# Clearing each layer's semaphores on GpSimd inside the following layer, with one barrier between two layers

## The chip, the cores and the metric

The kernel runs on one core of one Trainium2 chip. The metric is the time of one execution on the device, in microseconds. Before the change three runs took 1180.79, 1188.72 and 1182.0 us; their median is 1182.0 us.

A core has five engines, each with its own instruction queue: TensorE (PE in the profile; its weight loads have a row of their own, PEld), VectorE (DVE), ScalarE (ACT), GpSimd (POOL) and SyncE (SP, which here only starts DMAs). [...]

## What is computed

The reference is a stack of eight residual blocks on an input of 16 sequences x 128 tokens x 128 features: four times an attention over a context (16 heads), each followed by a feed-forward block of another kind. Each block reads the normalised rows of what the blocks before left:

```
x = x + _L0_xattn_ref(_layernorm(x), ctx_1024, mask, ...)   # masked attention
x = x + _L0_ffn_ref(_layernorm(x), ...)                      # top 2 of 8 experts, 2 iterations
x = x + _L1_xattn_ref(_layernorm(x), ctx_1024, ctx_1024, ...)  # a temperature per head
x = x + _L1_ffn_ref(_layernorm(x), ...)                      # top 1 of 14 experts
x = x + _L2_xattn_ref(_layernorm(x), ctx_1024, ...)          # self, then cross attention
x = x + _L2_ffn_ref(_layernorm(x), ...)                      # product keys
x = x + _L3_xattn_ref(_layernorm(x), ctx_1024, ctx_1024, ...)  # causal attention
x = x + _L3_ffn_ref(_layernorm(x), ...)                      # gated low-rank layers
return x
```

## The kernel before

x stays in on-chip memory throughout. `build` calls one function for each block, in the order of the reference; the first attention calls `first_layernorm` ahead of itself, so there are nine stages: the first row norm, l0, l0f, l1, l1f, l2, l2f, l3, l3f (the names that the tiles carry as a prefix; all attentions use the tile prefix `l_`).

Each stage has this frame:

- `with cleared_semaphores(nc) as new_semaphore` (line 33). It hands out the stage's semaphores. When the stage is left, GpSimd clears them all (`nc.clear_and_free_semaphores(taken)`, line 42) and gives their numbers back, and then all five engines meet in a barrier (`nc.all_engine_barrier()`, line 43).
- Inside it `nc.Block()`. Each engine gets its own instruction list for the stage. When the block is left, all five engines meet in a barrier too. Its instructions carry the line of the stage's `with` statement in the trace: 215 for the first row norm, 266 for l0 and l3, 1225 for l0f, 603 for l1, 1726 for l1f, 2161 for l2, 2460 for l2f, 1990 for l3f.

A barrier goes like this: each engine executes a DRAIN, which waits until its earlier instructions are done, and raises one semaphore; POOL waits for four of these, then raises a second semaphore, and each other engine goes on when it sees that one. I call this last step the release.

So two barriers stand between two stages, with the clear between them. The second is there because the next stage takes the same semaphore numbers again, and none may count on one before it is zero.

What stands around the boundary is much the same for all stages. A stage ends in DVE's last row statistics (`RowStats.take`, lines 120 and 123). The next begins with `RowNorm`: DVE normalises rows (line 179) and PE turns them (line 188). Three rows are normalised on ACT (line 193), for which POOL first makes `away` (lines 165 and 168). POOL also makes the last four rows' scale (lines 128 and 131). Behind that POOL's own work for the stage starts: the setting of buffers to constants (`MEMSET`, lines 342 to 347 in l0 and l3, 680 to 685 in l1, 1308 to 1313 in l0f, 2717 and 2718 in l2f), an addition (line 2240) in l2, the scatter of rows (line 1798) in l1f, and nothing in l3f. In l0, which has its row norm in a stage of its own, these MEMSETs come first.

In l1f, POOL scatters rows to DRAM, copies expert weights (line 1805), waits till the results are in DRAM, and gathers them back with 16 indirect DMAs (line 1811).

Of the kernel before, what the change touches and what calls it, by code (L numbers as in the profile page):

```python
# [31 lines left out]
@contextmanager  # L32
def cleared_semaphores(nc):

    taken = []

    def new_semaphore(name):
        taken.append(nc.alloc_semaphore(name=name))
        return taken[-1]

    yield new_semaphore
    nc.clear_and_free_semaphores(taken)
    nc.all_engine_barrier()
# [94 lines left out]
class RowNorm:  # L138
# [24 lines left out]
    def pool(self, pool):  # L163
        m, known = self.m, slice(0, RowStats.KNOWN)
        self.nc.gpsimd.tensor_tensor(self.away[:, known], m["row_mean_var"][:, known, 0], m["row_rstd"][:, known],
                                     ALU.mult).then_inc(self.away_made, 1)
        pool.wait_ge(self.away_made, 1)
        self.nc.gpsimd.tensor_scalar(self.away[:, known], self.away[:, known], -1.0, None, ALU.mult) \
            .then_inc(self.away_made, 1)
        self.row_stats.scale(pool, RowStats.KNOWN, B, rms=self.rms_gain is not None).then_inc(self.rstd_made, 1)  # L170

# [40 lines left out]
def first_layernorm(nc, m, tag, meanwhile):  # L212

    x, xnT, identity = m["x"], m["xnT"], m["identity"]
    with cleared_semaphores(nc) as new_semaphore, ExitStack() as ctx:
# [43 lines left out]
def cross_attention(nc, m, w, tag, meanwhile, masked_keys=False, causal=False, first=None, keys=None):  # L259
# [6 lines left out]
    with cleared_semaphores(nc) as new_semaphore, ExitStack() as ctx:  # L266
# [71 lines left out]
        def _(pool):  # L338
            if norm is not None:
                norm.pool(pool)  # L340
            for r in range(2):
                nc.gpsimd.memset(neg_max[r][:, :], 0.0).then_inc(ready, 1)
# [255 lines left out]
def tempered_attention(nc, m, w, tag, meanwhile):  # L598
# [4 lines left out]
    with cleared_semaphores(nc) as new_semaphore, ExitStack() as ctx:  # L603
# [577 lines left out]
def refine_experts(nc, m, w, tag, meanwhile):  # L1181
# [43 lines left out]
    with cleared_semaphores(nc) as new_semaphore, ExitStack() as ctx:  # L1225
# [492 lines left out]
def top1_experts(nc, m, w, tag, meanwhile, keys_ahead, values_ahead, last_keys, ahead_of):  # L1718
# [7 lines left out]
    with cleared_semaphores(nc) as new_semaphore, ExitStack() as ctx:  # L1726
# [67 lines left out]
        def _(pool):  # L1794
# [6 lines left out]
            for j in range(NT):  # L1801
                e = pool.value_load(tile_u[0:1, j:j + 1], min_val=0, max_val=E - 1)
                if j >= RING:
                    pool.wait_ge(y_stored, j - RING + 1)
                nc.gpsimd.tensor_copy(held[j % RING][:, :], w["experts"][:, bass.ds(e, 1), :].rearrange("p a f -> p (a f)")) \
                    .then_inc(fetched, 1)
            pool.wait_ge(scattered_early, 16 * EARLY)
# [175 lines left out]
def gated_lora(nc, m, w, tag, meanwhile):  # L1983
# [6 lines left out]
    with cleared_semaphores(nc) as new_semaphore, ExitStack() as ctx:  # L1990
# [160 lines left out]
def two_attentions(nc, m, w, tag, meanwhile, fold_of, keys_ahead, values_ahead):  # L2151
# [9 lines left out]
    with cleared_semaphores(nc) as new_semaphore, ExitStack() as ctx:  # L2161
# [291 lines left out]
def product_keys(nc, m, w, tag, meanwhile):  # L2453
# [6 lines left out]
    with cleared_semaphores(nc) as new_semaphore, ExitStack() as ctx:  # L2460
# [9 lines left out]
        spare, taken = m["spare"], [m["fold"].shape[1]]  # L2470
# [549 lines left out]
def build(nc, dram, where, out):  # L3020

    with ExitStack() as ctx:
# [37 lines left out]
        m["out"] = out  # L3060
# [43 lines left out]
        for name, layer, tag, options, meanwhile in run:  # L3104
# [12 lines left out]
            layer(nc, m, by_group[tag], tag, meanwhile, **options)  # L3117

# [16 lines left out]
```

## Time and profile before

| | us |
|---|---|
| three runs | 1180.79, 1188.72, 1182.0 |
| their median | 1182.0 |
| the profiled execution | 1187.32 |
| its span, first to last instruction | 1185.6 |
| busy in it: PE | 948.0 |
| DVE | 740.0 |
| ACT | 583.8 |
| POOL | 414.4 |

The span is what the trace covers; 1.7 us of the profiled execution lie around it. Busy time is the sum of an engine's instructions; barrier, semaphore and DRAIN instructions are not in it. They are found by asking for the line that issued them.

### The profile page before, as it was taken

What the parts mean: (1) busy time and instruction counts of PE and PEld (TensorE: products, weight loads), DVE (VectorE), ACT (ScalarE), POOL (GpSimd) and SP (SyncE); (2) the same over time, 40 slices, a digit from 0 to 9 for tenths busy, and PEclk for the clock granted to TensorE, in tenths of its full rate; (3) what the DMA queues carried; (4) which work ended last, traced back from release to release, by engine and by line L of the source; (5) the groups of instructions that cost most, each with busy time, mean ns of one, the idle gap of its engine ahead of it and who ended that gap; (6) DMA issues with size and microseconds to landing.
All of it is one profiled execution on the core that took longest, in us unless ns stands there. A gap on an engine that the chain in (4) does not pass through costs nothing. (4 is left out here: it accounts for less than half of the span.)

```text
span 1185.6 us, 26637 instructions
## 1 busy us (share of the span) xinstructions
PE 948.0 (80%) x10747; PEld 617.9 (52%) x10777; DVE 740.0 (62%) x2026; ACT 583.8 (49%) x956; POOL 414.4 (35%) x426
## 2 busy tenths in 40 slices
PE   3999799998999986998798781777556677479997
PEld 1577433443333433677676381445345555446776
DVE  3587747557455564654375233478899999636764
ACT  3365365535555344554563460377555555325442
POOL 4230300000000011676201656246578878623340
PEclk9799699998999998999898796899778987789997
DMA  6000000000000007000000132100000000000001
GB/s 268 1 3 2 19 1 0 1 1 0 1 1 1 0 1 288 10 2 3 2 3 2 36 110 56 72 1 1 1 2 2 2 2 3 2 1 2 2 2 37
DMA packets 15434, 27.95 MB, mean 24 GB/s; under 512 B 1104, under 2 KB 13264, under 8 KB 14544
## 3 DMA queue, kind: packets, MB, share of 16 engines
q1 hardware_dynamic: 14288, 24.14, 5.7%
q0 software_dynamic: 1024, 2.10, 0.6%
q8 instruction: 87, 1.43, 0.5%
q14 instruction: 35, 0.29, 0.1%
HBM read 20.33 MB, written 5.90 MB: 22 GB/s over the span
## 5 line engine op out<-in xcount | busy, mean ns | idle before, releaser
L1324 PE MATMUL l0f_ctl<-l1f_in,l0f_in 128*128 128x512 f32 x320 | 145.7, 599 | 0.5
L128 POOL TENSOR_SCALAR row_var_eps<-row_mean_var 128x12 f32<-128x12 f32 (+2 forms) x16 | 3.7, 230 | 358.5 <-DVE row_mean_var L123 357.7
L548 DVE TENSOR_REDUCE l_neg_max<-l_ring 128x4 f32<-128x512 f32 x128 | 82.1, 684 | 66.1 <-PE l_ring L410 65.6
L507 ACT ACTIVATE l_probs<-l_scores 128x1024 f32<-128x1024 f32 x64 | 65.6, 1025 | 82.2 <-PE l_scores L418 82.2
L2663 ACT COPY l2f_blocks_sb<-l2f_right_t_sb 32x1024 f32<-32x1024 f32 x64 | 66.8, 1044 | 68.2 <-DVE l2f_right_t_sb L2804 33.8
L1324 PEld LDWEIGHTS l0f_ctl<-l1f_in,l0f_in 128*128 128x128 f32 x320 | 61.7, 193 | 71.5 <-issue 70.2
L2593 PE MATMUL l2f_given_ps<-l2f_blocks_sb,l2f_left_t_sb 128*32 128x128 f32 x1024 | 47.8, 364 | 33.1 <-ACT l1f_in L2669 22.6
L698 POOL TENSOR_TENSOR l_squares<-l_exps 128x1024 f32<-128x1024 f32 x32 | 60.6, 1895 | 29.8 <-ACT l_exps L953 29.8
L2593 PEld LDWEIGHTS l2f_given_ps<-l2f_blocks_sb,l2f_left_t_sb 128*32 128x32 f32 x1024 | 42.8, 150 | 47.1 <-issue 46.9
L1045 DVE TENSOR_REDUCE l_neg_max<-l_scores 128x8 f32<-128x1024 f32 x32 | 39.2, 1225 | 43.4 <-PE l_scores L750 43.4
L368 POOL TENSOR_SCALAR_AFFINE_SELECT l_probs<-l_probs 128x1024 f32<-128x1024 f32 x32 | 35.0, 1094 | 64.1 <-ACT l_probs L507 64.1
L1597 DVE TENSOR_SCALAR l0f_halt<-l0f_halt 128x512 f32<-128x512 f32 x8 | 3.4, 427 | 78.8 <-ACT l0f_halt L1483 78.8
L1590 DVE SCALAR_TENSOR_TENSOR l1f_in<-l0f_index,l0f_in,l0f_hidden 128x512 f32<-128x512 bf16 x64 | 43.5, 747 | 12.3 <-ACT l0f_index L1464 11.1
L2743 POOL TENSOR_TENSOR l2f_factors_sb<-l2f_factors_sb,l1f_in 128x512 f32<-128x512 f32 x32 | 48.0, 1500 | 0.0
L953 ACT ACTIVATE l_exps<-l_scores 128x1024 f32<-128x1024 f32 x32 | 32.8, 1025 | 30.0 <-PE l_scores L756 29.8
L410 PE MATMUL l_ring<-l_k_heads,l_q_all 32*128 32x256 f32 x256 | 41.0, 441 | 7.9 <-issue 3.2
L1324 PE MATMUL l0f_work<-xnT,l0f_in 128*128 128x512 f32 (+2 forms) x88 | 45.0, 684 | 1.3 <-ACT xnT L204 0.7
L750 PE MATMUL l_scores<-l_k_heads,l_q_all 32*128 32x256 f32 x256 | 36.8, 402 | 10.0 <-DVE l_neg_max L1045 8.3
L2569 PE MATMUL l2f_sim_ps<-l1f_in,xnT 128*128 128x512 f32 x32 | 21.6, 764 | 28.8 <-DVE l1f_in L2772 28.8
L1446 ACT ACTIVATE l0f_hidden<-l0f_work,l0f_in 128x512 f32<-128x512 f32 (+1 forms) x40 | 27.3, 686 | 29.0 <-PE l0f_work L1324 29.0
L992 ACT ACTIVATE l_exps<-l_scores 128x1024 f32<-128x1024 f32 x32 | 31.0, 1021 | 20.7 <-PE l_scores L837 20.7
L756 PE MATMUL l_scores<-l_q_all,l_k_heads 32*128 32x128 f32 x512 | 37.7, 286 | 1.8 <-ACT l_exps L953 1.8
(458 smaller groups left out, 2610.2 us busy)
## 6 DMA issues: line engine op xcount, KB each, us to landing
l1f_in<-in_l1f SPq DMA_DIRECT2D x1, 4580.0 KB, 13.4
l0f_in<-in_l0f SPq DMA_DIRECT2D x1, 2302.5 KB, 8.9
l0f_in<-in_l2f SPq DMA_DIRECT2D x1, 2080.5 KB, 18.7
l1f_in<-in_l2u SPq DMA_DIRECT2D x1, 2048.0 KB, 8.6
sorted_rows<-first_in SPq DMA_DIRECT2D x1, 1856.0 KB, 11.2
l1f_sorted<-sorted_rows SPq DMA_DIRECT2D x7, 256.0 KB, 4.6
expert_rows<-l1f_sorted SPq DMA_DIRECT2D x7, 256.0 KB, 2.2
x_in<-in_x SPq DMA_DIRECT2D x1, 1024.0 KB, 5.0
```

The source lines that it names most:

```text
L410: ins1 = mm(score_bank(b, half, g)[:, :, t, :], q_all[r, b, t, :], k_heads[r, b, t, :, :], start=not causal, stop=True, skip_group_check=True)
L507: nc.scalar.activation(probs[c % 2][:, 2 * pair:2 * pair + 2], scores2[:, :, :, :, :], ACT.Exp, scale=SCORE_SCALE).then_inc(exp_done, 1)
L548: ring.free(V.tensor_reduce(out, score_bank(b, half, g), AX.X, ALU.max, negate=True), ("score", b, half, g))
L698: nc.gpsimd.tensor_tensor(squares[c % 2][:, pair], e, e, ALU.mult).then_inc(squared, 1)
L750: ins1 = mm(scores1[:, g, :, t, :], q_all[r, b, t, :], k_heads[r, b, t, :, :], start=True, stop=True, skip_group_check=True)
L756: ins2 = mm(scores2[:, g, j, t, :], k_heads[r, c, t, j, :], q_all[r, c, t, :], start=True, stop=True, skip_group_check=True)
L1045: V.tensor_reduce(out, scores1[:, :, :, :, :].rearrange("p g j t s -> p (g j) t s"), AX.X, ALU.max, negate=True).then_inc(max_taken, 1)
L1324: return nc.tensor.matmul(out, lhs, rhs, start=start, stop=stop)
L1590: ins = STT(chosen[c % 2][:, k, p, :], index[k][:, c % 2, :], w["row_expert"][:, p:p + 1], hidden[c % 2][:, p, :], ALU.is_equal, ALU.mult)
L2593: ins = mm(given_ps[K * j:K * j + K, s, :, :], left_t[b % 2][:, 8 * j + s, :], blocks[:, 8 * j + s, :, :], start=True, stop=True)
L2663: A.copy(blocks[rows, :, u, :], right_t[rows, :, :]).then_inc(blocks_made, 1)
L2743: TT(value, value, kept[:, side, :, :], ALU.mult).then_inc(cut_made, 1)
```

## The change

A stage's semaphores are no longer cleared when the stage is left, and the barrier of line 43 goes. The list is kept in `m["semaphores_to_clear"]`, and the next stage clears it on POOL: in the stages with a row norm of the usual kind at the end of `RowNorm.pool`, behind the four small instructions, and in l0 ahead of the MEMSETs. The next stage has other semaphore numbers, since the old ones aren't free before that. The last stage's are cleared after it, with one barrier behind, as before. l1f gets one more `drain` on POOL, between the copies of the expert weights and the wait for the DRAM writes.

```
-def cleared_semaphores(nc):
+def cleared_semaphores(nc, m):
     ...
     yield new_semaphore
-    nc.clear_and_free_semaphores(taken)
-    nc.all_engine_barrier()
+    assert not m["semaphores_to_clear"]
+    m["semaphores_to_clear"] = taken
+
+
+def clear_last_layers_semaphores(nc, m):
+    nc.clear_and_free_semaphores(m["semaphores_to_clear"])
+    m["semaphores_to_clear"] = []
 ...
         self.row_stats.scale(pool, RowStats.KNOWN, B, rms=self.rms_gain is not None).then_inc(self.rstd_made, 1)
+        clear_last_layers_semaphores(self.nc, m)
 ...
             if norm is not None:
                 norm.pool(pool)
+            else:
+                clear_last_layers_semaphores(nc, m)
             for r in range(2):
                 nc.gpsimd.memset(neg_max[r][:, :], 0.0).then_inc(ready, 1)
 ...
                 nc.gpsimd.tensor_copy(held[j % RING][:, :], w["experts"][:, bass.ds(e, 1), :].rearrange("p a f -> p (a f)")) \
                     .then_inc(fetched, 1)
+            nc.gpsimd.drain()
             pool.wait_ge(scattered_early, 16 * EARLY)
 ...
-        m["out"] = out
+        m["out"], m["semaphores_to_clear"] = out, []
 ...
             layer(nc, m, by_group[tag], tag, meanwhile, **options)
+        clear_last_layers_semaphores(nc, m)
+        nc.all_engine_barrier()
```

The eight `with cleared_semaphores(nc)` lines become `with cleared_semaphores(nc, m)`. The line numbers of the changed file are larger by 5 or more.

POOL's instructions from the end of l0 to the first work of l0f, before (a branch is the jump out of one block or into the next, ISA is the clear of a range of semaphores; DRAINs and barrier instructions are not listed):

```order
L266 UNCONDITIONAL_BRANCH
L42 ISA
L1305 UNCONDITIONAL_BRANCH
L165 TENSOR_TENSOR l0f_away<-row_mean_var,row_rstd 128x12
L168 TENSOR_SCALAR l0f_away<-l0f_away 128x12
L128 TENSOR_SCALAR row_var_eps<-row_mean_var 128x4
L131 TENSOR_TENSOR row_rstd<-row_var_eps,first_in 128x4
L1308 MEMSET l0f_choice 128x2048
```

and of the change:

```order
L272 UNCONDITIONAL_BRANCH
L1313 UNCONDITIONAL_BRANCH
L170 TENSOR_TENSOR l0f_away<-row_mean_var,row_rstd 128x12
L173 TENSOR_SCALAR l0f_away<-l0f_away 128x12
L133 TENSOR_SCALAR row_var_eps<-row_mean_var 128x4
L136 TENSOR_TENSOR row_rstd<-row_var_eps,first_in 128x4
L47 ISA
L1316 MEMSET l0f_choice 128x2048
```

The clear moved past the four small instructions, ahead of the first MEMSET. No other instruction of these changed its place.

POOL's instructions from the gather of l1f into l2, before:

```order
L1811 DMA l1f_rows<-expert_rows,l1f_place_u 128x128 x16
L128 TENSOR_SCALAR row_var_eps<-row_mean_var 128x12
L131 TENSOR_TENSOR row_rstd<-row_var_eps,first_in 128x12
L1726 UNCONDITIONAL_BRANCH
L42 ISA
L2223 UNCONDITIONAL_BRANCH
L165 TENSOR_TENSOR l_away_sb<-row_mean_var,row_rstd 128x12
L168 TENSOR_SCALAR l_away_sb<-l_away_sb 128x12
L128 TENSOR_SCALAR row_var_eps<-row_mean_var 128x4
L131 TENSOR_TENSOR row_rstd<-row_var_eps,first_in 128x4
L2240 TENSOR_TENSOR l_last_b_sb<-l_in 128x128
```

and of the change:

```order
L1820 DMA l1f_rows<-expert_rows,l1f_place_u 128x128 x16
L133 TENSOR_SCALAR row_var_eps<-row_mean_var 128x12
L136 TENSOR_TENSOR row_rstd<-row_var_eps,first_in 128x12
L1734 UNCONDITIONAL_BRANCH
L2232 UNCONDITIONAL_BRANCH
L170 TENSOR_TENSOR l_away_sb<-row_mean_var,row_rstd 128x12
L173 TENSOR_SCALAR l_away_sb<-l_away_sb 128x12
L133 TENSOR_SCALAR row_var_eps<-row_mean_var 128x4
L136 TENSOR_TENSOR row_rstd<-row_var_eps,first_in 128x4
L47 ISA x2
L2249 TENSOR_TENSOR l_last_b_sb<-l_in 128x128
```

The same move, and the clear is now of two ranges: the numbers of a stage no longer follow one another without a gap. Over the whole program there is one range in l0 and l0f, three in l2f, and two in each of the others and at the end. On PE, DVE, ACT and SP no listed instruction changes its place.

## Rows read from the trace of the kernel before

**Rows 1.** The page: span, then busy time and share of the span by engine.
```profile
span 1185.6 us, 26637 instructions
PE 948.0 (80%) x10747; PEld 617.9 (52%) x10777; DVE 740.0 (62%) x2026; ACT 583.8 (49%) x956; POOL 414.4 (35%) x426
```

**Rows 2.** Line 42, then 43, whole span: ns min/median/max, first to last start.
```profile
L42 POOLq EVENT_SEMAPHORE_RANGE_CLEAR  x9: 73/243/348, 17.1 to 1185.2; - x9
L43 POOLq EVENT_SEMAPHORE  x18: 17/17/17, 17.2 to 1185.5; - x18
L43 POOLq DRAIN  x9: 34/34/40, 17.2 to 1185.3; - x9
L43 DVEq EVENT_SEMAPHORE  x9: 21/21/21, 17.4 to 1185.5; - x9
```

**Rows 3.** Boundary l0 to l0f: block's release, line 42, second release.
```profile
L266 DVEq EVENT_SEMAPHORE  x1: 21/21/21, 130.1 to 130.1; - x1
L42 POOLq EVENT_SEMAPHORE_RANGE_CLEAR  x1: 178/178/178, 130.3 to 130.3; - x1
L43 DVEq EVENT_SEMAPHORE  x1: 21/21/21, 130.7 to 130.7; - x1
```

**Rows 4.** The same three at the boundary l2 to l2f.
```profile
L2161 DVEq EVENT_SEMAPHORE  x1: 21/21/21, 839.5 to 839.5; - x1
L42 POOLq EVENT_SEMAPHORE_RANGE_CLEAR  x1: 348/348/348, 839.7 to 839.7; - x1
L43 DVEq EVENT_SEMAPHORE  x1: 21/21/21, 840.3 to 840.3; - x1
```

**Rows 5.** The same three at the boundary first row norm to l0.
```profile
L215 DVEq EVENT_SEMAPHORE  x1: 21/21/21, 16.9 to 16.9; - x1
L42 POOLq EVENT_SEMAPHORE_RANGE_CLEAR  x1: 73/73/73, 17.1 to 17.1; - x1
L43 DVEq EVENT_SEMAPHORE  x1: 21/21/21, 17.4 to 17.4; - x1
```

**Rows 6.** Timeline, l0 to l0f: start, us, what [idle before <-releaser].
```profile
129.72 0.18 DVE L123 BATCH_NORM_AGGREGATE row_mean_var<-row_stats 128x2 f32<-128x6 f32 x1
130.81 3.95 DVE L179 TENSOR_SCALAR l1f_in<-x_in,row_mean_var,row_rstd 128x128 f32<-128x128 f32 x9 [0.91 <-PEq L43]
...
131.21 2.37 PE L188 MATMUL l0f_ctl<-first_in,l1f_in 128*128 128x128 f32 x9 [2.52 <-DVE l1f_in L179]
```

**Rows 7.** Timeline of POOL in l0f, then line 1570's wait on DVE.
```profile
136.03 0.13 POOL L1313 MEMSET l0f_half<- 128x1 f32 x1
144.80 1.65 POOL L1318 TENSOR_TENSOR l0f_gap_exp<-common_in,l0f_gap 128x8 f32<-128x8 f32 x1 [8.64 <-DVE l0f_gap L1566]
L1570 DVEq EVENT_SEMAPHORE  x2: 21/21/21, 145.0 to 186.9; - x2
```

**Rows 8.** Waits of POOL: line waited for: us in total, times, longest us.
```profile
POOL l_probs L368 <- ACT l_probs L507: 64.1, 32, 12.6
POOL l_rstd_sb L2230 <- DVE l_var_eps_sb L2426: 47.6, 10, 27.7
POOL l_max_all L690 <- DVE l_neg_max L1045: 18.3, 2, 13.4
POOL sorted_rows L1798 <- DVE l1f_place_u L1949: 16.3, 1, 16.3
POOL l1f_in L2723 <- DVE l1f_in L2758: 4.3, 1, 4.3
```

**Rows 9.** Timeline of l3's start: POOL's last MEMSETs, PE's first scores.
```profile
1050.86 0.17 POOL L347 MEMSET l_v<- 128x16 f32 x2
1055.55 0.38 PE L395 MATMUL l_ring<-common_in 128*128 128x512 bf16 x1 [1.04 <-ACT l_q_all L495]
```

**Rows 10.** Timeline of POOL in l1f, then DRAINs at the block's end (line 1726).
```profile
711.18 2.24 POOL L1805 COPY l1f_held<-l1f_in 128x642 f32 x3 [0.55 <-DVE l1f_sorted L1972]
718.90 1.01 POOL L1811 DMA_INDIRECT l1f_rows<-expert_rows,l1f_place_u  x1 [5.47 <-DMA expert_rows<-l1f_sorted]
L1726 POOLq DRAIN  x1: 5042/5042/5042, 739.0 to 739.0; - x1
L1726 DVEq DRAIN  x1: 406/406/406, 742.4 to 742.4; - x1
```

**Rows 11.** DRAINs of POOL at other blocks' ends.
```profile
L266 POOLq DRAIN  x2: 2379/2380/2382, 120.7 to 1154.6; - x2
```

**Rows 12.** Windows: us, then busy us of PE, PEld, DVE, ACT, POOL, PEclk, DMA, GB/s.
```profile
131.00:149.00 18.00, 15.10 (x63) 7.77 (x64) 16.38 (x67) 7.17 (x12) 6.38 (x9) 0.50 0.10 30
150.00:168.00 18.00, 15.57 (x44) 6.00 (x44) 9.87 (x15) 13.05 (x22) 0.00 (x0) 1.00 0.00 1
```

More of the change, by code:

```diff
@@ L214, in first_layernorm @@
     x, xnT, identity = m["x"], m["xnT"], m["identity"]
-    with cleared_semaphores(nc) as new_semaphore, ExitStack() as ctx:
+    with cleared_semaphores(nc, m) as new_semaphore, ExitStack() as ctx:
         def sem(name):
@@ L265, in cross_attention @@
     KINDS, AHEAD = len(kinds), 5 if keys is None else T
-    with cleared_semaphores(nc) as new_semaphore, ExitStack() as ctx:
+    with cleared_semaphores(nc, m) as new_semaphore, ExitStack() as ctx:
         def sb(name, shape):
@@ L602, in tempered_attention @@
     PARTS = ((0, 12), (12, B))
-    with cleared_semaphores(nc) as new_semaphore, ExitStack() as ctx:
+    with cleared_semaphores(nc, m) as new_semaphore, ExitStack() as ctx:
         def sb(name, shape):
@@ L1223, in steps @@
                 yield n, it, c, g, r, part
-    with cleared_semaphores(nc) as new_semaphore, ExitStack() as ctx:
+    with cleared_semaphores(nc, m) as new_semaphore, ExitStack() as ctx:
         def sb(name, shape, dt=F32):
@@ L1725, in top1_experts @@
     x, xnT, identity = m["x"], m["xnT"], m["identity"]
-    with cleared_semaphores(nc) as new_semaphore, ExitStack() as ctx:
+    with cleared_semaphores(nc, m) as new_semaphore, ExitStack() as ctx:
         def sb(name, shape, dt=F32):
@@ L1989, in gated_lora @@
     x, xnT, identity = m["x"], m["xnT"], m["identity"]
-    with cleared_semaphores(nc) as new_semaphore, ExitStack() as ctx:
+    with cleared_semaphores(nc, m) as new_semaphore, ExitStack() as ctx:
         def sb(name, shape):
@@ L2160, in two_attentions @@
              sorted((n + SKEW * c, c, name, a) for n, (name, a) in enumerate(STAGES) for c in range(NCH))]
-    with cleared_semaphores(nc) as new_semaphore, ExitStack() as ctx:
+    with cleared_semaphores(nc, m) as new_semaphore, ExitStack() as ctx:
         def sb(name, shape, dt=F32):
@@ L2459, in product_keys @@
     x, xnT, identity = m["x"], m["xnT"], m["identity"]
-    with cleared_semaphores(nc) as new_semaphore, ExitStack() as ctx:
+    with cleared_semaphores(nc, m) as new_semaphore, ExitStack() as ctx:
         def sb(name, shape):
```

## The prediction

> **What bounds the kernel now.** I read the page first, for what fills the span. No engine does: PE is busy 948.0 of 1185.6 us, DVE 740.0, POOL only 414.4 [rows 1]. The stages run strictly one after another, and each hands over through a point where all five engines stand still. So next I asked for the lines of that point, 42 (the clear) and 43 (the second barrier). Each occurs nine times [rows 2], once behind each stage. Then I looked at single boundaries.
>
> At the end of l0 DVE gets the release of the block's own barrier at 130.1 and the release of the second barrier at 130.7; between them lies a clear of 178 ns [rows 3]. DVE's last statistics start at 129.72 and its first work of l0f at 130.81, after 0.91 us of idling [rows 6]. Both are on the path: the statistics were the last work of l0, and the row norm that PE, ACT and all else of l0f wait for starts right behind the release. So at a boundary the time from the first release to the second adds to the span one to one, whichever engine was last before and whichever is first after.
>
> **What the change does, part by part.**
>
> *Removed: the time from release to release, at eight boundaries.* It has a fixed part and the clear. Three boundaries give 130.7 - 130.1 = 0.6 us with a clear of 0.178 [rows 3], 840.3 - 839.5 = 0.8 with 0.348 [rows 4], and 17.4 - 16.9 = 0.5 with 0.073 [rows 5]. Less the clear that leaves 0.42, 0.45 and 0.43 us, so 0.43 fixed. These three have the smallest and the largest clear of the nine, whose median is 0.243 [rows 2]. The removed time is 8 x (0.43 + 0.243) = 5.4 us. The starts are given to 0.1 us; if each difference were off by 0.1 in the same direction, the sum would be 4.6 or 6.2.
>
> The records of the removed instructions alone come to far less: one clear of 0.243, a DRAIN of 0.034, two semaphore instructions of 0.017 on POOL and the release of 0.021 [rows 2] make 0.33 us a boundary, 2.7 us for eight. The rest is time in which no record runs. The Trainium skill, Perfetto Trace Analysis, section Sequencer-only Instruction, says that a record holds only the execution, and that the wait and the spreading of a semaphore's new value to all engines are outside it. By that rule too the price is the one from release to release, and by records alone 2.7 us; the trace agrees with the rule, with 0.6 us between releases where the records make up about half.
>
> *Moved: the clears, onto POOL inside the next stage.* Each holds POOL for its own time, a DRAIN ahead of it, and a start: from the first release to the end of the clear it was about 0.2 + 0.348 us at the largest [rows 4], which I take as 0.55 us at most for one range, and somewhat more for two or three. POOL was itself released 0.5 to 0.8 us earlier, so in time its later work starts about where it did; in distance to its consumers, which all moved up, it is some 0.5 us late. What hides it, stage by stage:
> - l0f: the last MEMSET starts at 136.03, and the wait of DVE for it is executed at 145.0; POOL's next real work waits 8.64 us for DVE [rows 7].
> - l1, l1f, l2: behind the first small instructions POOL idles 13.4, 16.3 and 27.7 us for DVE, the longest waits of these three rows [rows 8].
> - l2f: 4.3 us of idle time for DVE [rows 8].
> - l3: the last MEMSETs start at 1050.86, and the first scores that need them at 1055.55, held up by ACT [rows 9]; that is 4.5 us. POOL's first causal mask then idles 12.6 us [rows 8].
> - l0's MEMSETs are like l3's, and l3f has no POOL work behind it.
>
> The smallest cover is 4.3 us against 0.5, so I cost the move at nothing. With the cover gone it would be up to 0.55 us each, 4.4 us for eight.
>
> *Added: the `drain` in l1f.* POOL's last copy ends at 711.18 + 2.24 = 713.4 (the three are back to back), and its next instruction starts at 718.90 because of a DMA [rows 10]. That is 5.5 us of cover. A DRAIN of POOL at a block's end takes 2.38 us behind a long instruction [rows 11] and 5.04 us in l1f behind the indirect DMAs [rows 10]. Bounds: nothing, if it only waits for the copies; 5.04 us, still under the cover. I take nothing. There is a possible gain in it. The DRAIN at l1f's end lasts from 739.0 to 744.0, while DVE's is over at 742.8 [rows 10], so this one boundary waits 1.2 us for POOL. If part of that long DRAIN is old business of the scatter that the new drain settles earlier, up to 1.2 us more is won. Nothing in the trace speaks for the scatter rather than the gather, which is the nearer in time, so I take 0 here too.
>
> *Added: a second range at the end of the program.* It is on the path. Between 0.07 and 0.35 us by the clears [rows 5, 4], but the total of semaphores is the same, so the low end: 0.1 us.
>
> **The sum.** 5.4 - 0.1 = 5.3 us. The profiled execution took 1187.32 us (span 1185.6 and 1.7 around it), so it would take 1182.0. That execution was 5.3 us above the median of the runs, 1182.0; taken from this median the sum gives 1176.7. The three runs and the profiled one have a mean of 1184.7, which gives 1179.4. Between these I take 1178.
>
> **The rivals.**
>
> *A. The clear isn't hidden.* A clear in the midst of a stage may hold up the semaphores that the other engines are using just then, or the jump into the next block, which so far stood behind a second wait, shows up. By the rows the first costs at most the clears themselves, 8 x 0.243 = 1.9 us, and the gain would be 3.4: 1178.6 to 1181.3 by the two bases. For it: the clear now falls into the row norm, where three engines hand rows to each other. Against it no row bears either, since before the change nothing else ran beside a clear. For the jump, DVE's first work of l0f starts 0.1 us behind the release, the jump included [rows 3, 6]. The Trainium skill, Runtime: NRT & Kernel Launch, section Instruction fetch mechanics, says that a taken branch to code that is not yet fetched stalls until it is; by that rule l0f's code was there in time, and what a miss would cost no row here shows.
>
> *B. A bonus from l1f.* Up to 1.2 us more: 1175.5 to 1178.
>
> *C. PE's clock takes it back, and the kernel is not faster, or slower.* In l0f's first 18 us the granted clock is 0.50 (the lower level, 1.2 GHz), and in the 18 us from 150 it is 1.00 (2.4 GHz), with PE busy 15.1 and 15.6 us [rows 12]; ahead of it PE had idled 2.52 us at the boundary [rows 6]. Which work falls under the low level depends on when it starts, and eight boundaries shift against that. One low stretch of that kind more costs half of its PE time, 7.5 us, less the 5.3: 1184 from the median, 2 us slower than before. It decides from 10.6 us of PE time on the path at the lower level. The Trainium skill, TensorE: Matmul & The Clock Gate, section Part 1, says that the gate runs freely, not in step with the kernel's start; by it the outcome would differ from run to run. The three runs of before differ by 7.9 us with nothing changed, about that size. Against a lasting loss: the pauses of PE at the boundaries get shorter, not longer.
>
> *D. Nothing.* If the second barrier's time were hidden behind something else. Rows 6 speak against it: nothing runs between. 1182.
>
> **How the numbers follow.** The forecast (4.5 to 6 us won) has 0.6, A 0.14, B 0.08, C 0.13, D 0.05. The likeliest case alone gives 1176 to 1180, by 4.5 from the upper base and 6 from the lower. The range goes down to 1173 (B, with a base a few us better, as the runs vary) and up to 1185 (C's 1184, A and D inside). 1% of the time, 11.8 us, is about what a measurement of this kernel can tell from no change. The sum is 0.45% and even its upper bound of 6.2 with B's 1.2 is 0.6%; faster by over 1% needs luck with the clock on top: 0.04. Slower by over 1% needs C several times: 0.02. Within 1%: 0.94.
>
> **What would show it.** Right: line 43's instructions occur only once, at the end; DVE's idle time before line 179's successor falls from 0.91 to about 0.3 us at l0f, and likewise by 0.5 to 0.8 at the seven others; the clears stand beside DVE's and PE's row norm; POOL still idles before its first long work of each stage. Wrong for A: row norms that take longer from the first to the last row, or gaps on PE and DVE at the time of a clear. B: a DRAIN at l1f's end under 4 us. C: a low stretch of the clock that is longer or newly there, with matmuls of the same line at twice their duration. The prediction is wrong if a stage, measured from release to release, changes by more than some tenths of a us at the same clock, or if POOL's waits of 4.3 us turn out to be zero.

## The result and the profile after

The changed kernel takes 1175.93 us (median of 8 runs, 1172.04 to 1179.3); the kernel before took 1184.25 us beside it (8 runs, 1180.79 to 1190.57). The ratio is 0.992, with a 95% interval of 0.9896 to 0.9944. The forecast was 1178.0 in a range of 1173 to 1185, within 1% of before: both hold. The gain was forecast at 5.3 us and is 8.3 in these runs by the medians (6.6 to 12.3 by the interval), and larger in later ones. Three later runs (1198.67 and 1200.71 us of the kernel before, 1199.29 of e2) fell in a slower state of the chip and, like one outlier of e5, are in no ratio and no mean below. The profiled execution took 1176.08 us, with a span of 1174.0.

The page of the changed kernel, span and busy time by engine (before: [rows 1]):

```profile
span 1174.0 us, 26596 instructions
PE 953.2 (81%) x10777; PEld 622.7 (53%) x10777; DVE 735.9 (63%) x2026; ACT 583.3 (50%) x956; POOL 413.9 (35%) x426
```

No engine has less to do: the counts are the same, but for 30 matmul records on PE that are missing in the trace before (its weight loads are 10777 in both). The first thing to look for is the second barrier. (A semaphore is a small counter that one instruction raises and another waits for.) In the changed kernel each boundary inside the program has only the block's own release. Here the boundary l0 to l0f, which answers to [rows 3, 6]: first the release (line 272) and the clear on POOL (line 47), from the views of these lines (ns min/median/max, first to last start).

```profile
L272 DVEq EVENT_SEMAPHORE  x1: 21/21/21, 128.6 to 128.6; - x1
L47 POOLq DRAIN  x1: 1202/1202/1202, 129.7 to 129.7; - x1
L47 POOLq EVENT_SEMAPHORE_RANGE_CLEAR  x1: 178/178/178, 130.9 to 130.9; - x1
```

Then the timelines (start, us, what, idle before and its releaser) of DVE with its last statistics and first row norm, of PE's first work, and of POOL's first instructions of l0f.

```profile
128.23 0.18 DVE L128 BATCH_NORM_AGGREGATE row_mean_var<-row_stats 128x2 f32<-128x6 f32 x1
128.74 5.08 DVE L185 TENSOR_SCALAR l1f_in<-x_in,row_mean_var,row_rstd 128x128 f32<-128x128 f32 x13 [0.33 <-PEq L272]
...
129.14 2.74 PE L194 MATMUL l0f_ctl<-first_in,l1f_in 128*128 128x128 f32 x12 [1.94 <-DVE l1f_in L185]
...
129.74 1.04 POOL L136 TENSOR_TENSOR row_rstd<-row_var_eps,first_in 128x4 f32<-128x4 f32 x1
131.18 1.80 POOL L1316 MEMSET l0f_choice<- 128x2048 f32 x1 [0.40 <-issue]
...
134.34 0.10 POOL L1321 MEMSET l0f_half<- 128x1 f32 x1
142.50 1.64 POOL L1326 TENSOR_TENSOR l0f_gap_exp<-common_in,l0f_gap 128x8 f32<-128x8 f32 x1 [8.06 <-DVE l0f_gap L1574]
```

DVE idles 0.33 us instead of 0.91 [rows 6], and PE 1.94 instead of 2.52: 0.58 us each, which is what stood between the two releases. The clear now runs at 130.9 for 0.18 us, beside DVE's row norm. POOL's last MEMSET starts 134.34 - 128.6 = 5.7 us behind the release, before 136.03 - 130.7 = 5.3 [rows 3, 7]; POOL still waits 8.06 us after that. The move is hidden.

The timeline merges DVE's 13 rows into one line. The view of the line itself has their shortest, median and longest, of the changed kernel (line 185) and of the kernel before (line 179):

```profile
L185 DVE TENSOR_SCALAR l1f_in<-x_in,row_mean_var,row_rstd x13: 342/346/2018, 128.7 to 133.3; 128x128 f32<-128x128 f32 x13
L179 DVE TENSOR_SCALAR l1f_in<-x_in,row_mean_var,row_rstd x13: 342/347/2083, 130.8 to 135.6; 128x128 f32<-128x128 f32 x13
```

So a few rows take far longer than 0.35 us, up to 2.02 us, in both kernels. They lie beside POOL's large MEMSET (1.80 us from 131.18 on), not beside the clear: the nine rows that start before the MEMSET take 0.34 to 0.35 us each, the one during which the clear runs among them. What in the MEMSET holds DVE up no run separates. From the release the last row starts 133.3 - 128.6 = 4.7 us later, and before 135.6 - 130.7 = 4.9.

Now the whole span, by stages. Each window below runs from the release that opens a stage to the block's release that ends it (start:end, us, busy us and count by engine, granted clock, DMA share, GB/s). The kernel before; l0, l0f, l1, l1f, l2, l2f, l3, l3f:

```profile
17.40:130.10 112.70, 98.89 (x1440) 72.16 (x1440) 68.48 (x176) 56.01 (x82) 28.73 (x28) 0.92 0.07 27
130.70:450.30 319.60, 294.97 (x709) 119.17 (x720) 190.11 (x381) 162.92 (x234) 11.50 (x12) 0.94 0.01 2
451.00:640.10 189.10, 163.39 (x3048) 126.02 (x3048) 104.70 (x255) 100.89 (x148) 73.61 (x64) 0.93 0.13 48
640.80:744.20 103.40, 63.22 (x369) 51.48 (x369) 33.88 (x120) 39.08 (x91) 55.97 (x67) 0.73 0.20 58
745.00:839.50 94.50, 64.81 (x408) 44.48 (x412) 66.35 (x269) 57.67 (x157) 42.38 (x51) 0.90 0.07 23
840.30:1046.40 206.10, 135.06 (x3136) 110.38 (x3136) 185.03 (x553) 105.28 (x144) 151.19 (x144) 0.83 0.01 2
1047.00:1160.10 113.10, 104.14 (x1489) 74.18 (x1504) 71.41 (x189) 51.71 (x80) 45.27 (x48) 0.95 0.01 2
1160.80:1185.00 24.20, 19.06 (x132) 17.18 (x132) 11.22 (x35) 6.60 (x15) 1.82 (x4) 0.85 0.13 45
```

The changed kernel, the same eight:

```profile
16.80:128.60 111.80, 99.70 (x1440) 72.53 (x1440) 68.47 (x176) 56.09 (x82) 28.87 (x28) 0.94 0.07 29
128.60:445.40 316.80, 291.97 (x720) 117.36 (x720) 189.85 (x381) 162.67 (x234) 11.44 (x12) 0.96 0.01 2
445.40:631.80 186.40, 161.71 (x3048) 124.67 (x3048) 104.00 (x255) 100.82 (x148) 73.83 (x64) 0.94 0.14 49
631.80:734.40 102.60, 62.68 (x369) 51.61 (x369) 33.91 (x120) 38.98 (x91) 55.81 (x67) 0.74 0.20 58
734.40:830.10 95.70, 70.61 (x412) 49.38 (x412) 63.72 (x269) 57.62 (x157) 42.29 (x51) 0.84 0.06 23
830.10:1037.90 207.80, 139.79 (x3136) 114.44 (x3136) 184.59 (x553) 105.42 (x144) 151.01 (x144) 0.81 0.01 2
1037.90:1149.10 111.20, 103.22 (x1504) 72.71 (x1504) 71.29 (x189) 51.48 (x80) 44.95 (x48) 0.98 0.01 2
1149.10:1173.30 24.20, 18.99 (x132) 17.11 (x132) 11.22 (x35) 6.59 (x15) 1.82 (x4) 0.85 0.12 44
```

Read two things. First, after's windows touch each other. Before there are gaps: 16.9 to 17.4, 130.1 to 130.7, and so on. By exact starts they sum to 5.35 us. Second, the stages themselves sum to 1162.7 before and 1156.5 after, 6.2 us less. Where a stage got shorter its clock is higher (l0 0.92 to 0.94, l0f 0.94 to 0.96, l1 0.93 to 0.94, l3 0.95 to 0.98), and where it got longer its clock is lower (l2 0.90 to 0.84, l2f 0.83 to 0.81). Only l1f stands out: 0.8 us shorter at much the same clock. So three questions were open: what l1f's added `drain` does, whether the barrier or the clear is the price, and whether the clock's share comes from the change or from chance.

### The profile page after: what moved, and what is told of

Its sections match the earlier page's. It is cut to its first block and busy times, and to the rows that moved or that the text cites. A ratio compares the mean times of both kernels' runs of the same rounds, so it can differ in the third digit from the quotient of the medians.

```text
span 1174.0 us, 26596 instructions
## 1 busy us (share of the span) xinstructions
PE 953.2 (81%) x10777; PEld 622.7 (53%) x10777; DVE 735.9 (63%) x2026; ACT 583.3 (50%) x956; POOL 413.9 (35%) x426
```

## The experiments

In all of them but e9 the time is the median of 5 to 12 runs, against the kernel before on the same chip; e9 has one run, 1175.74 us. Its medians there were 1189.17 us (24 runs; e1 to e4), 1188.97 (31 runs; e5 to e8) and 1189.29 (18 runs; e9 to e11), some 5 us more than in the first runs. So ratios are compared, not times. No two of the ratios of the changed kernel and of its variants without an added barrier (0.9881 to 0.9922) are clear of one another. "Stage" times are from release to release in the profile of each.

| run | what | us | ratio, 95% | boundaries | l0 | l0f | l1 | l1f | l3 |
|---|---|---|---|---|---|---|---|---|---|
| e5 | before, unchanged | 1187.23 | 0.9970 (0.9937 to 1.0003) | 5.35 | 112.8 | 319.5 | 189.2 | 103.2 | 113.3 |
| e2 | before + drain | 1191.53 | 1.0013 (0.9983 to 1.0044) | 5.35 | 113.8 | 316.8 | 185.3 | 101.8 | 120.8 |
| e3 | change - drain | 1180.89 | 0.9913 (0.9881 to 0.9946) | 0 | 113.8 | 317.9 | 189.3 | 103.8 | 112.3 |
| e4 | change + 1 barrier | 1183.18 | 0.9954 (0.9931 to 0.9978) | 2.66 | 111.7 | 316.5 | 189.3 | 102.2 | 112.7 |
| e6 | change + 2 barriers | 1184.55 | 0.9973 (0.9948 to 0.9997) | 5.62 | 111.8 | 316.6 | 192.1 | 102.4 | 113.0 |
| e1 | change, again | 1175.37 | 0.9881 (0.9841 to 0.992) | 0 | 111.6 | 316.4 | 189.6 | 102.5 | 112.4 |
| e11 | change, again | 1179.24 | 0.9922 (0.9895 to 0.9949) | 0 | 111.8 | 317.6 | 185.3 | 102.6 | 112.8 |
| e7 | change + 10 matmuls in l0 | 1176.26 | 0.9900 (0.9866 to 0.9933) | 0 | 108.3 | 317.8 | 189.1 | 102.6 | 112.3 |
| e8 | change + 46 matmuls | 1178.27 | 0.9917 (0.9892 to 0.9942) | 0 | 107.6 | 318.1 | 189.4 | 104.0 | 112.0 |
| e10 | change - last barrier | 1177.55 | 0.9901 (0.9862 to 0.994) | 0 | 112.7 | 317.6 | 188.5 | 102.7 | 112.5 |

### e1, e5 and e11: the two kernels again, unchanged

> The changed kernel once more, beside the kernel before on the same chip. The measured gain was 8.3 us (1184.25 to 1175.93, interval 6.6 to 12.3). The sum from the trace is 5.35 us between the two releases at eight boundaries, 1.2 us at the end of l1f where the DRAIN of POOL became shorter, less 0.1 at the end: 6.4 us. Theory 1 (the sum is all there is): 6.4 us, the rest was scatter of the runs. Theory 2 (something inside the stages is faster too, such as a higher clock of PE): 8 us or more again, and single stages shorter from release to release by more than 0.5 us at the same granted clock.

> The kernel before, unchanged, with a profile of its own. So far its runs spread over 18.6 us (1180.1 to 1198.7), the changed kernel's over 7.3 us (1172.0 to 1179.3). Theory 2 (the time of a stage follows how long the low clock of TensorE lay on it, and the kernel before catches more of it): the stages differ from the first profile of before only where their low stretches differ, by about 0.3 us per us of low clock in l0 (113.8 us with 20.7 us low against 111.8 with 13.7), and the ratio to itself is 1.00. Theory 1 (stages have one time, up to 0.5 us): all stages within 0.5 us of the first profile.

> The change once more, unchanged, with a profile of its own. Theory 1 (the clock's low stretches fall differently from run to run and make up the differences in the stages): the stages from release to release differ from the two profiles that there are of it by up to 3 us each, l1f's final DRAIN is 3.717 us again, all boundaries have one release. Rival (the sum of the changed instructions is all there is): every stage within 0.3 us of the earlier profiles. The ratio to before should be 0.988 to 0.994 by the first, 0.995 to 0.996 by the second.

By the expectations, e1 (0.9881, 13.8 us beside its own runs of before) came out as theory 2 said, more than the sum of 6.4, but no stage was shorter at the same clock, which that theory also asked for. e5's stages stayed within 0.5 us of the first profile, as theory 1 said. e11's ratio is inside the range of its theory 1, but l1 differs by more than the 3 us that it allowed.

Three profiles of the changed kernel differ in l1 by 4.3 us (186.4, 189.6, 185.3), in l0f by 1.2, in l3 by 1.6 and in l2f by 1.8 (207.8, 206.0, 206.0), with nothing changed. Boundaries, l1f (102.5 to 102.6) and the end (0.70) repeat to 0.1 us. The two profiles of the kernel before agree within 0.3 us in every stage, which is chance too, since its times spread more than the changed kernel's. For e5 one run of 4876.74 us is an outlier without a cause that a row shows. The rest of e5 shows what a ratio can tell: the same kernel against itself gave 0.9970, with 1.0 just inside.

### e2 and e3: the drain alone, and the change without it

```
# e2, on the kernel before          # e3, on the changed kernel
                     .then_inc(fetched, 1)
+            nc.gpsimd.drain()      -            nc.gpsimd.drain()
             pool.wait_ge(scattered_early, 16 * EARLY)
```

> The kernel before with nothing but the added drain of POOL in l1f. Theory 1 (the new drain settles what the scatter left behind, and the DRAIN at the end of l1f then has only the gather's part): POOL's DRAIN at the end of l1f falls from 5.0 to 3.7 us, and the kernel is 1.2 us faster than before. Rival (the shorter DRAIN came from the removed clears and barriers, or varies from run to run): DRAIN 5.0 us, no change of the time.

> The changed kernel without the added drain. Theory 1: DRAIN of POOL at the end of l1f 5.0 us again, 1.2 us slower than the changed kernel, that is 5.2 us faster than before by the sum. Rival: DRAIN 3.7 us and the same time as the changed kernel.

POOL's DRAIN at l1f's end (line 1726 or 1734) in e2, then DVE's beside it, the release, and in another fence the same of e3:

```profile
L1726 POOLq DRAIN  x1: 3717/3717/3717, 733.2 to 733.2; - x1
L1726 DVEq DRAIN  x1: 404/404/404, 736.5 to 736.5; - x1
L1726 DVEq EVENT_SEMAPHORE  x1: 21/21/21, 737.1 to 737.1; - x1
```

```profile
L1734 POOLq DRAIN  x1: 5043/5043/5043, 736.3 to 736.3; - x1
L1734 DVEq DRAIN  x1: 404/404/404, 739.6 to 739.6; - x1
```

With the added drain 3.717 us, without it 5.043, in both frames (boundaries as before, or as in the change). In e3 POOL is done at 741.3 and DVE at 740.0, so the barrier waits 1.3 us for POOL; in e2 both are done at 736.9. The stage follows: 101.8 to 102.7 us in all profiles that have the drain and nothing else added in l1f (eight of them), 103.2 to 103.8 in all that don't. The cleanest pairs have the gather at the same place behind the release. Without and with the drain it is 103.2 (e5) and 101.8 (e2) in the frame of before, 103.8 (e3) and 102.6 (the change) in the changed one. So the added drain is worth 1.3 and 1.2 us there. The full 1.33 us by which POOL's DRAIN got shorter shows only in the first: in the second DVE comes out last.

Across the frames l1f is 0.4 to 0.9 us longer in the changed one, with the drain and without. The moved clears are not the cause: POOL's first scatter starts 18.4 to 18.5 us behind the release in all of them. PE's last matmul ends 75.0 to 75.2 us behind it in the frame of before and 75.4 to 75.8 in the changed one, and the gather follows it. The granted clock from 40 to 50 us behind the release was 0.83 in the first and 0.66 in the second. That fits, but no run separates it.

Over the whole kernel e2 is no faster than before: in its profile 7.5 us went in l3 (120.8 against 113.3), where the clock was low for longer. Here e2's l3, 0.90 granted against 0.95 before:

```profile
1040.70:1161.90 121.20, 112.06 (x1504) 76.08 (x1504) 74.43 (x189) 51.56 (x80) 44.92 (x48) 0.90 0.01 2
```

One such stretch hides the drain's 1.2 us and any other term of the sum. So the half of e2's theory on the DRAIN came true, and the half on the time can't be told. e3 still gains 0.9% (0.54 to 1.19%), more than its 5.2 us of boundaries (0.44%): the drain is not needed for most of the gain, and the boundaries' records don't make up all of it.

### e9: what the long DRAIN consists of

```
             for b in range(B):
+                if b == 8:
+                    nc.gpsimd.drain()
                 nc.gpsimd.indirect_dma_start(rows[:, b, :], None, y_dram[:, :],
```

> The change with one more DRAIN of POOL in l1f, between the 8th and the 9th of the 16 gathering indirect DMAs. Theory 1 (each indirect DMA that no DRAIN has followed yet costs the next DRAIN the same time: 5.042 us without the drain behind 32 of them, 3.717 us with it behind 16, so 0.083 us each and 2.39 us besides): the DRAIN at l1f's end takes 2.39 + 8 x 0.083 = 3.05 us. Rival (only the scatter leaves something to be settled, the gather nothing): 3.72 us as in the change. The stage itself may get a little longer, since POOL issues its last eight gathers behind a DRAIN of 2 to 3 us; DVE's additions wait for these.

The DRAIN at l1f's end:

```profile
L1734 POOLq DRAIN  x1: 3054/3054/3054, 732.3 to 732.3; - x1
```

POOL's timeline: the eighth and the ninth gather, and the last instruction of the stage.

```profile
718.71 0.94 POOL L1822 DMA_INDIRECT l1f_rows<-expert_rows,l1f_place_u  x1 [0.30 <-issue]
722.28 0.94 POOL L1822 DMA_INDIRECT l1f_rows<-expert_rows,l1f_place_u  x1 [2.63 <-issue]
...
732.31 2.31 POOL L136 TENSOR_TENSOR row_rstd<-row_var_eps,first_in 128x12 f32<-128x12 f32 x1
```

At l1f's end it is 3.054 us, as theory 1 said to the hundredth. The DRAIN's record begins together with POOL's last instruction, which takes 2.31 us. What is left beyond it is 2.73 us with 32 indirect DMAs behind no drain, 1.41 with 16, and 0.74 with 8: 83 ns for each, and under 0.1 us besides. The scatter and the gather leave the same. The drain behind the copies agrees: 1.36 us beyond the last copy, for 16.

The drain in the midst of the gather does not agree. Its record:

```profile
L1821 POOLq DRAIN  x1: 8715/8715/8715, 712.9 to 712.9; - x1
```

It ends at 712.9 + 8.7 = 721.6, and the eighth indirect DMA ended at 718.71 + 0.94 = 719.65. That is 1.9 us beyond, where eight times 83 ns make 0.7. So the 83 ns are the price where the transfers are done, and a DRAIN right behind an indirect DMA costs more. What it waits for there is open; from issue to landing these DMAs take 2.5 us in the same trace, which would reach 718.7 + 2.5 = 721.2. The drain held POOL for 2.63 - 0.30 = 2.3 us, and since DVE's last additions wait for the gather, l1f took 105.0 us, 2.4 more. Behind the copies, where the change has it, it lies in 5.4 us of waiting for a DMA.

### e4, e6 and e10: barriers without a clear, and no barrier at the end

```
# e4, on the changed kernel; e6 has the line twice
     yield new_semaphore
+    nc.all_engine_barrier()
     assert not m["semaphores_to_clear"]
# e10, on the changed kernel
         clear_last_layers_semaphores(nc, m)
-        nc.all_engine_barrier()
```

> The changed kernel with a second barrier put back at every stage's end, without a clear before it; the clears stay inside the following stages. It splits the gain: the clear by itself was 1.98 us over eight boundaries (0.07 to 0.35 each). Theory 1 (the time from release to release is fixed part plus clear): a barrier without a clear costs about 0.3 us by the steps of the second barrier in the trace, 2.4 us for eight, so this kernel is 2.4 us slower than the changed one and some 4 us faster than before. Rival (any second barrier costs the 0.43 us of fixed time or more): 3.4 us or more slower than the changed one.

> The changed kernel with two barriers without a clear put back at each stage's end (one cost 2.66 us between releases over eight boundaries and the end, and 7.8 us of time). Direct price of two: 5.3 us, so 1180.7 by the sum alone. Theory 2a (waits at the boundaries have a second price through the clock, in proportion): twice 7.8, 1191 us. Theory 2b (the price through the clock is a step or a matter of chance): the second barrier costs its 2.7 us more only, 1184 to 1187 us.

> The change without the barrier at the very end of the program; POOL still clears the last semaphores. From the release of l3f's block to the last instruction it took 0.70 us in the change and 0.57 before. The fixed part of 0.43 should go and the clears stay: 0.25 to 0.3 us. That is 0.4 us of 1176, below what the times can tell, so the verdict comes from the end of the trace; the ratio to before should stay at 0.988 to 0.994.

DRAINs and release of one such barrier in e4, at l0's end, and how long DVE's first row norm of l0f waited for it:

```profile
L42 POOLq DRAIN  x1: 41/41/41, 128.9 to 128.9; - x1
L42 PEldq DRAIN  x1: 13/13/13, 129.0 to 129.0; - x1
L42 DVEq EVENT_SEMAPHORE  x1: 21/21/21, 129.2 to 129.2; - x1
  DVE l1f_in L186: 0.7, 1
```

A barrier alone costs 0.33 us from release to release at each of eight boundaries (2.66 in all), two cost 0.66 at most of them (5.62 in all), although the records of one sum to under 0.1. DVE waits 0.7 us instead of 0.33 (last row). The old boundary of 0.45 to 0.79 us is this 0.33 and the clear with its start. The Trainium skill, Perfetto Trace Analysis, section Sequencer-only Instruction, says that a record leaves out the wait and the spreading of a semaphore's value; the rows agree. In e10 the end, from the last block's release, fell from 0.70 to 0.41 us, where 0.25 to 0.3 was expected: it lost 0.3, the price of a barrier by e4, and not the fixed part of 0.43. In the time that can't be told.

In the times e4 keeps about half of the gain (0.46%, 5.5 us) and e6 a quarter (0.27%, 3.2 us). Both keep l1f's 1.2 us. With the end of the program (1.35 and 1.38 us instead of 0.70) the barriers put back 3.3 and 6.3 us. Of the change's 6.4 us (5.35 + 1.2 - 0.13) e4 should have kept 3.1 and e6 0.1. e4's interval (2.6 to 8.2 us) holds that, e6's (0.4 to 6.2) just doesn't. Twice the barriers cost 2.3 us more in the ratios (5.5 - 3.2), where the records make 3.0. By the times e4 was 7.8 us slower than e1, which ran on the same chip (1183.18 and 1175.37). 3.3 of them are the barriers. The mean clock of e4's runs is lower too (0.8926 against 0.9056), and e1 has the lowest of the changed kernel's ratios. e6's 1184.55 is what its theory 2b said (1184 to 1187), and far from 2a's 1191.

### e7 and e8: matmuls that keep the clock up

```
# e7, in l0 ahead of PE's wait for POOL's first MEMSETs
             if masked_keys:
+                for _ in range(10):
+                    mm(scores2[:, 0, 0, 0, :], identity[:, :], identity[:, :], start=True, stop=True)
# e8: these, and 8 to 10 more of the kind at the ends of l0, l3, l1f and l2
```

The added matmuls write to a bank that is not in use yet, and nothing reads them.

> The changed kernel with ten matmuls more on PE in l0, in a pause of 3.2 us in which PE waits for the first scores' keys; their results are not used. Theory 2: the low stretch of 13.7 to 20.5 us that begins 9 to 12 us into l0 goes or gets shorter, l0 falls from 111.6 to 113.8 us to 108 to 110, and the kernel is 2 to 4 us faster than the changed one, though PE has more work. Theory 1 (the clock in l0 makes no difference): no change or slower by the fillers.

> As the run before, with eight to ten such matmuls more on PE ahead of the boundaries behind l0, l1f, l2 and l3, while PE waits there for DVE; again their results are not used. It fills the pauses without shortening any barrier. Theory 2: the low stretches at the start of l0f, l2, l2f and l3f get shorter, and the kernel is faster than with the filler in l0 alone, by 1 to 4 us. Rival: these starts wait for DVE and ACT, not for PE, and nothing changes or the fillers delay the barrier.

The stretch from 28 to 42 us, first of the changed kernel:

```profile
28.00:42.00 14.00, 12.65 (x54) 6.84 (x54) 5.51 (x10) 1.37 (x2) 6.04 (x5) 0.51 0.00 1
```

then of e7, with all of l0 below it:

```profile
28.00:42.00 14.00, 10.63 (x82) 6.77 (x81) 8.38 (x14) 3.42 (x4) 6.15 (x5) 0.88 0.01 2
...
16.50:124.80 108.30, 97.83 (x1460) 73.26 (x1460) 68.32 (x176) 56.22 (x83) 28.93 (x28) 0.98 0.08 33
```

In these 14 us the clock goes from 0.51 to 0.88, PE gets through 82 matmuls instead of 54, and l0 takes 108.3 us instead of 111.8. The ten added ones (20 records of PE) ran before 28 us, from 23.9 to 26.3. So the clock is worth 3.5 us in this one stage, and a program that shifts by little can win or lose that. In the time of the kernel nothing of it is seen: 0.9900, with the changed kernel itself at 0.9881, 0.992 and 0.9922; and in e7's profile l0f (317.8) and l1 (189.1) stand at or beyond the long end of the unchanged kernel's spread (316.4 to 317.6 and 185.3 to 189.6). e8 holds the clock up most of all (0.917 in its profile, against 0.899 to 0.909) and is no faster. Its l1f took 104.0 us instead of 102.5 to 102.7, behind the fillers at its end, as its rival said. That a part of the higher mean clock lies on time in which PE did nothing but fill is likely, but not shown. Theory 2 of e7 held in l0 (108.3, where 108 to 110 was expected), and failed in the time, as e8's did.

## How much of the gain is the clock

Every run lists its span and its mean clock, so two sets can be compared beyond single profiles. These are the runs taken beside one another in the experiments: 82 of the kernel before, 17 of the changed kernel.

| | span, mean | clock, mean | time at the low level |
|---|---|---|---|
| before | 1186.5 | 0.8955 | 2 x (1 - 0.8955) x 1186.5 = 248 |
| changed | 1176.0 | 0.9018 | 2 x (1 - 0.9018) x 1176.0 = 231 |

The gain is 10.5 us, and the changed kernel spends 17 us less at the low level (1.2 GHz). Within the kernels, over 168 runs of nine programs, a span grows by 0.258 us with each us at the low level. By this slope 17 us are worth 4.4, and 6.1 (4.8 to 7.2) are left at an equal clock. The records make it 5.35 (the boundaries) - 0.13 (the end) + 1.2 (l1f) = 6.4. Without a slope, by runs of the same clock: between 0.900 and 0.9049 the mean span is 1181.2 before (15 runs) and 1176.0 changed (8 runs), 5.3 by the unrounded means. So the change is worth some 5 to 7 us at a given clock, and the other 4 to 6 us go with a higher clock on average. The slope is rough: it takes every low us for alike, wherever PE is waited for or not. The same reckoning leaves e3 8.2, e4 6.6 and e6 4.8 us, where their records make 5.2, 3.1 and 0.1. An error of 3 to 5 us in such a reckoning is thus possible, and the agreement of 6.1 with 6.4 proves little.

Better evidence comes from single stages. A stage can be compared where profiles of both frames happened to have the same granted clock in it. Times are from release to release:

| stage | clock | frame of before | changed frame |
|---|---|---|---|
| l0 | 0.91 | 113.8 (e2) | 113.8 (e3) |
| l0 | 0.92 | 112.7, 112.8 (before, e5) | 112.7, 111.8 (e10, e6) |
| l0f | 0.95 | 319.5 (e5) | 317.9 (e3) |
| l0f | 0.96 | 316.8 (e2) | 316.4 to 317.6 (seven profiles) |
| l1 | 0.92 | 189.2 (e5) | 189.3, 189.3, 189.6 (e3, e4, e1) |
| l1 | 0.93 | 189.1 (before) | 188.5 (e10) |
| l1 | 0.95 | 185.3 (e2) | 185.2, 185.3 (e9, e11) |
| l2 | 0.84 | 95.4 (e2) | 95.4 to 95.8 (change, e4, e6) |
| l2 | 0.90 | 94.6, 94.6 (before, e5) | 94.6 (e9) |
| l2f | 0.83 | 206.1 to 206.4 (before, e5, e2) | 205.9 to 206.5 (e1, e9, e10, e11) |
| l3 | 0.95 | 113.1 (before) | 113.0 (e6) |
| l3 | 0.97 | 113.3 (e5) | 112.7, 112.8 (e4, e11) |

These are all the pairs with the clock the same to two decimals, e7 and e8 with their added matmuls and the short l3f left out; l1f is treated with e2 and e3. All but two agree within 0.8 us, most of them within 0.4, and the two that don't (e6's l0, and l0f at 0.95) are 0.9 and 1.6 us shorter in the changed frame. The rest of the differences between stages, up to 4 us in l1, goes with the clock. So at an equal clock the moved clears lengthen no stage by an amount that these rows can show, and most of what was won beyond the boundaries and l1f lies in where the low stretches fall, as far as single profiles show it. One thing stays open beside this: e6 is 3.2 us faster than before (0.4 to 6.2), where its records make 0.1 and its mean clock is not higher but lower (0.8929 against 0.8955).

Why the changed kernel finds a higher clock stays open. It isn't the drain by itself (e2 has 0.8882 as its mean), and with barriers put back the clock falls (0.8926 in e4, 0.8929 in e6). That fits PE's shorter pauses at the boundaries, 1.94 against 2.52 us at l0f. But e3 has the short pauses and 0.8956, so they aren't enough. A single profile tells little here: e3 differs from the changed kernel in nothing ahead of l1f, and yet its profile has l0 at 113.8 us and a clock of 0.91, against 111.6 to 111.8 and 0.94 in the three of the changed kernel. No run separates a cause in the program from the mere shift of each stage's start.

## Why the prediction was right, step by step

The time and the verdict (within 1%) came as forecast, and the main mechanism is right. The closeness of the time is in part luck, as the last two points say, and one term failed.

- **The place** (a boundary adds its release-to-release time one to one, whoever was last): right. DVE's idle time went from 0.91 to 0.33 at l0f, as forecast ("about 0.3").
- **Removed, 5.4 us**: right, 5.35 by exact starts in two profiles. The clear (0.243, the median, where the mean of the eight is 0.25) and the fixed part (0.43, where 0.42 is left) were well sized. e4 splits the fixed part: 0.33 is the barrier.
- **The moved clears cost nothing**: right. POOL's MEMSETs come 0.4 us later behind the release in l0f (5.7 against 5.3) and 0.3 in l3 (below), and what needs them starts later still. Rival A, a hold-up of the others, would show in the row norm beside the clear; DVE's rows there take 0.34 to 0.35 us as before, and the long ones lie beside a MEMSET in both kernels.

```profile
1042.07 0.17 POOL L355 MEMSET l_v<- 128x16 f32 x2
...
1044.85 0.59 PE L403 MATMUL l_ring<-common_in 128*128 128x512 bf16 x2 [0.82 <-issue]
```

  The last MEMSETs of l3 start 1042.07 - 1037.9 = 4.2 us behind the release, before 3.9 [rows 9]. The cover shrank from 4.5 to 2.6 us, more by PE's earlier scores (7.0 us behind the release, before 8.5) than by the clear. The smallest cover, l2f's wait of 4.3 us, fell to 3.3, since three ranges are cleared there and hold POOL for 0.9 us, where the prediction had 0.55 for one and "somewhat more" for three; it is still covered:

```profile
840.10 0.41 POOL L2732 TENSOR_TENSOR l1f_in<-l1f_in 128x128 f32<-128x128 f32 x1 [3.34 <-DVE l1f_in L2767]
```

- **The drain in l1f, taken as 0, at most 1.2 us**: this is the term that was mis-sized. Rival B, with a chance of 0.08, came true in full. The rows of the changed kernel answer to [rows 10]: the added DRAIN (line 1815) and the DRAINs at the end (line 1734), then POOL's last copies and first gather.

```profile
L1815 POOLq DRAIN  x1: 2138/2138/2138, 704.1 to 704.1; - x1
...
L1734 POOLq DRAIN  x1: 3717/3717/3717, 730.4 to 730.4; - x1
L1734 DVEq DRAIN  x1: 408/408/408, 733.8 to 733.8; - x1
```

```profile
703.45 1.43 POOL L1813 COPY l1f_held<-l1f_in 128x642 f32 x2 [0.44 <-DVE l1f_sorted L1981]
710.31 1.01 POOL L1820 DMA_INDIRECT l1f_rows<-expert_rows,l1f_place_u  x1 [5.43 <-DMA expert_rows<-l1f_sorted]
```

  The added one ends at 706.2, 1.36 us behind the last copy and 4.1 ahead of the gather. The last one is 1.325 us shorter, and POOL and DVE are done together. At l1f's end the barrier had waited for POOL; DVE's idle time there fell by 2.0 us, 0.73 of them the second release:

```profile
734.48 1.62 DVE L185 TENSOR_SCALAR l_rows_sb<-x_in,row_mean_var,row_rstd 128x128 f32<-128x128 f32 x6 [0.33 <-PEq L1734]
```

```profile
745.06 1.11 DVE L179 TENSOR_SCALAR l_rows_sb<-x_in,row_mean_var,row_rstd 128x128 f32<-128x128 f32 x4 [2.33 <-PEq L43]
```

  (the first is the changed kernel, the second the kernel before). The step that failed was the reading of a 5.04 us DRAIN as something that belongs to the nearest work. It had 32 indirect DMAs behind no drain, and the same view had a POOL DRAIN of 2.38 with none [rows 11]: half of the difference, 1.33 us, belonged to the scatter. This also tripped the prediction's own sign of being wrong, a stage that changes by more than some tenths at the same clock: l1f fell by 0.8 us at 0.73 and 0.74.
- **The end, 0.1 us**: 0.13.
- **The clock, rival C** (one more low stretch takes 7.5 us back): the mechanism is there, as e2's l3 shows with 7.5 us, and as the 4.3 us of unchanged l1 stages do. But on average it went the other way, and some 4 to 6 us of the gain go with a higher clock. "Against a lasting loss: the pauses get shorter" pointed the right way, and a gain from it should have stood among the rivals. The Trainium skill, TensorE: Matmul & The Clock Gate, section Part 1, says that the gate runs freely; the spread between equal programs agrees (1172.04 to 1184.85 us in 25 runs of the changed kernel). A difference that lasts over 82 and 17 runs doesn't follow from it.
- **The base**: the first three runs of before had their median at 1182.0; over the 82 later ones it is 1188.3. The forecast from it, 1178, met 1175.93, and over all 25 runs 1177.3, because a low base and an underrated gain went against each other. That is luck. The case that was called likeliest, 4.5 to 6 us won, was missed: the sum of the records is 6.4. Where it fell short is the difference to before: 5.3 forecast, 8.3 in the runs beside it, 10.5 in the later ones. "Within 1%" held there too (0.992), but e1, taken later, lies at 0.9881.

## What to carry to other kernels

Price a boundary from release to release, not by its records, and ask who is last at each: where one engine's DRAIN ends later than the others', look at what it has to settle, and settle it earlier in a wait that it has anyway. Semaphores can be cleared in the next stage by an engine that waits there, if the next stage takes other numbers; then one barrier is enough. Where a merged line of the timeline hides how long its parts take, ask for the line itself. For changes of some us, compare stages at the same granted clock, over several profiles of each kernel, and take the base from many runs.

## What the runs showed of the hardware

- Each indirect DMA of POOL leaves 83 ns for POOL's next DRAIN (2.73, 1.41 and 0.74 us for 32, 16 and 8), once. A DRAIN right behind eight of them took 1.9 us beyond the last (e9).
- A barrier of all five engines with nothing to wait for takes 0.33 us, and two in a row 0.66 at most boundaries. A clear of a range took 68 to 348 ns.
- The record of POOL's DRAIN at l1f's end begins together with POOL's last instruction and contains it (2.31 of 3.717 us).
- DVE's row norm in l0f took 0.34 to 0.35 us a row, and up to 2.02 and 2.08 us beside a MEMSET of 1.80 us on POOL, in both kernels.
- Ten matmuls of no use kept the clock at 0.88 instead of 0.51 over 14 us and made a stage 3.5 us shorter, and yet the kernel was no faster.
